# Idle bf16 matmuls moved around the last chunk's projection, and a cast of x1 given to ScalarE

## The reference

```
qkv = x @ w_qkv;  q, k = rope(rmsnorm(q)), rope(rmsnorm(k))
o   = softmax(q k^T / sqrt(8)) v
x   = layernorm(x + o @ w_proj + b_proj)                    # called x1 in the kernel
h   = silu((x @ w1) * s1) * ((x @ w2) * s2)                 # 128 -> 512
h   = gelu((h @ h1) * t1);  h = gelu((h @ h2) * t2)         # 512 -> 512, twice
out = layernorm(x + (h @ w3) * s3)                          # 512 -> 128
```

## Time and profile before

| | |
|---|---|
| three runs | 388.29, 390.14, 392.93 us; median 390.14 us |
| the profiled execution, its own time | 389.85 us |
| its span, first to last instruction | 388.1 us |
| mean granted TensorE clock over the span | 0.976 |
| busy share of the span | PE 87%, ACT 79%, DVE 52%, PEld 35%, POOL 5% |
| chain that ended last | PE 60%, ACT 17%, DVE 12%, issue 9% |

### The profile page before, as it was taken

One profiled execution on the slowest core, in us unless ns is written; L12 is line 12 of the kernel. 1 busy time (PEld: TensorE's weight loads), 2 busy tenths in 40 slices (PEclk: granted clock), 3 DMA queues, 4 the chain that ended last, 5 costly groups with the idle time before them and its releaser, 6 DMA issues.

```text
span 388.1 us, 6219 instructions
## 1 busy us (share of the span) xinstructions
PE 338.2 (87%) x2093; PEld 136.5 (35%) x2098; DVE 202.5 (52%) x397; ACT 306.1 (79%) x347; POOL 18.4 (5%) x21
## 2 busy tenths in 40 slices
PE   8976488878799999998999989998999899969980
PEld 3533111111132244533322444433223535425750
DVE  1899927101145754354556634455477153665754
ACT  2566399999999989797999888889998987852430
POOL 2300000000010000001100000011000000021001
PEclk9999699999999999999999999999999999988997
DMA  7998933123033030020302300303031100000001
GB/s 246 345 375 276 380 128 96 32 66 98 5 93 93 6 98 0 19 79 2 123 29 68 96 0 0 96 0 125 0 96 52 45 0 0 0 27 0 0 2 32
DMA packets 16201, 31.33 MB, mean 81 GB/s; under 512 B 1522, under 2 KB 5106, under 8 KB 16178
## 3 DMA queue, kind: packets, MB, share of 16 engines
q1 hardware_dynamic: 15938, 30.23, 23.8%
q0 software_dynamic: 240, 0.79, 0.5%
HBM read 19.21 MB, written 9.44 MB: 74 GB/s over the span
## 4 chain that ended last, share of the span: by engine, by line
PE 60%; ACT 17%; DVE 12%; issue 9%; ACTq 0%; POOLq 0%; DVEq 0%; POOL 0%
PE ps L456 20%; ACT probs L718 16%; PE ps L503 14%; PE ps L443 10%; PE ps L493 4%; PE ps L584 4%; DVE ffn L898 2%; PE ps L537 2%; DVE probs L805 2%; DVE parts L794 2%; PE ps L632 1%; PE ps L616 1%; PE ps L416 1%; PE ps L473 1%; DVE x_lo L873 1%
## 5 line engine op out<-in xcount | busy, mean ns | idle before, releaser
L718 ACT ACTIVATE probs<-ps 128x1024 f32<-128x1024 f32 x256 | 241.3, 1051 | 29.8 <-PE ps L443 29.7
L456 PE MATMUL ps<-probs,va 128*9 128x512 f32 x1024 | 130.3, 598 | 14.3 <-ACT probs L718 12.7
L443 PE MATMUL ps<-qa,ka 32*128 32x512 f32 x512 | 74.5, 501 | 11.7 <-ACT probs L718 7.0
L443 PEld LDWEIGHTS ps<-qa,ka 32*128 32x128 f32 x512 | 29.9, 184 | 108.7 <-ACT probs L718 68.7
L898 DVE TENSOR_SCALAR ffn<-ps,col 128x512 f32<-128x512 f32 x36 | 27.0, 750 | 55.1 <-PE ps L503 50.9
L503 PE MATMUL ps<-g_hi,w_hi 128*128 128x512 f32 x108 | 45.4, 421 | 2.5 <-DVE ffn L898 2.5
L503 PE MATMUL ps<-g_lo,w_hi 128*128 128x512 f32 x108 | 42.4, 392 | 0.0
L456 PEld LDWEIGHTS ps<-probs,va 128*9 128x9 f32 x1024 | 17.8, 89 | 62.3 <-ACT probs L718 32.5
L835 DVE STREAM_TRANSPOSE o_tok<-ps 128x512 f32<-128x512 f32 x15 | 10.7, 716 | 44.8 <-PE ps L456 44.8
L503 PEld LDWEIGHTS ps<-g_hi,w_hi 128*128 128x128 f32 x108 | 20.2, 187 | 15.4 <-DVE ffn L898 4.3
L873 DVE TENSOR_TENSOR g_lo<-ffn,g_hi 128x512 fp32r<-128x512 f32 x36 | 24.9, 692 | 1.2
(11 more groups left out here) (103 smaller groups left out, 290.6 us busy)
## 6 DMA issues: line engine op xcount, KB each, us to landing
ka<-k_scr SPq DMA_DIRECT2D x16, 512.0 KB, 4.1
qa<-q_scr SPq DMA_DIRECT2D x16, 256.0 KB, 4.1
q_scr<-parts SPq DMA_DIRECT2D x6, 512.0 KB, 6.4
k_scr<-parts SPq DMA_DIRECT2D x6, 512.0 KB, 6.7
va<-v_all SPq DMA_DIRECT2D x16, 144.0 KB, 4.5
ffn<-in_h SPq DMA_DIRECT2D x2, 1024.0 KB, 8.7
xT<-in_x_t SPq DMA_DIRECT2D x4, 256.0 KB, 4.9
q_scr<-rope SPq DMA_DIRECT2D x2, 512.0 KB, 7.1
```

What stands on the lines that cost most here:

```text
L443: mm = pe.matmul(s_tile(u)[:, i, :], ka[rows, slot, kt * P:(kt + 1) * P], qa[rows, slot, :], start=True, stop=not shifted)
L456: mm = pe.matmul(ps[32 * h:32 * h + VW, O_BANK, :], va[:, g % 2, kt, h, :], probs[:, step % 4, h, :], start=(kt == 0), stop=(kt == KT - 1))
L718: nc.scalar.activation(probs[:, step % 4, 2 * pair:2 * pair + 2, :], s_tile(u), ACT.Exp).then_inc(exp_done, 1)
```

## The change

The idle matmuls are spread over six places in place of two: `KEEP_WARM = (5, 6, 2, 10, 2, 3)`. Five go ahead of the last value matmuls, six behind them, two behind the first half of the projection, ten behind its second half (ahead of the turn of x1, where 14 were), two behind the first half of the turn, three behind its second. The wait on `mix_free` that stood behind the projection now stands ahead of the last value matmuls. The cast into `x_hi` goes from DVE to ACT, behind the preload of the Silu table; DVE waits for it (`last_x_high`) and does the subtraction alone. `G_SPLIT` is still counted up by DVE's subtractions.

```diff
-KEEP_WARM = (14, 6)
+KEEP_WARM = (5, 6, 2, 10, 2, 3)
...
+        last_x_high = sem("last_x_high")
...
-                def turned(step, bank0, src):
+                def turned(step, bank0, src, after=(0, 0)):
 
                     for hf in range(2):
                         pe.wait_ge(last_given, step + hf + 1)
                         for i in range(HT):
                             mm = pe.transpose(ps[:, bank0 + hf, i * P:(i + 1) * P], src(hf * HT + i), ident[:])
                         mm.then_inc(last_ready, 1)
-
+                        keep_warm(after[hf])
+
+                pe.wait_ge(mix_free, MIX_CHUNK * (NCH - 1) + MIX_FIRST)
+                keep_warm(KEEP_WARM[0])
                 values(c, STEPS - 1)
+                keep_warm(KEEP_WARM[1])
                 for hf in range(2):
                     pe.wait_ge(last_given, G_ATTN + hf + 1)
                     for i in range(HT):
                         mm = pe.matmul(ps[:, 4 + hf, i * P:(i + 1) * P], attnT[:, (hf * HT + i) * P:(hf * HT + i + 1) * P], wp[:],
                                        start=True, stop=True)
                     mm.then_inc(last_ready, 1)
-                pe.wait_ge(mix_free, MIX_CHUNK * (NCH - 1) + MIX_FIRST)
-                keep_warm(KEEP_WARM[0])
-                turned(G_X, 0, lambda i: x1[:, i, :])
-                keep_warm(KEEP_WARM[1])
+                    keep_warm(KEEP_WARM[2 + hf])
+                turned(G_X, 0, lambda i: x1[:, i, :], KEEP_WARM[4:6])
                 pe.wait_ge(last_given, G_SPLIT + 2)
...
             act.preload_act_table(ACT.Silu)
+            for hf in range(2):
+                act.wait_ge(last_ready, R_X + hf + 1)
+                nc.scalar.copy(x_hi[:, hf * HC:(hf + 1) * HC], ps[:, hf, 0:HC]).then_inc(last_x_high, 1)
...
             for hf in range(2):
-                dve.wait_ge(last_ready, R_X + hf + 1)
-                split(cb, ps[:, hf, 0:HC], half_of(x_hi, hf), half_of(x_lo, hf)).then_inc(last_given, 1)
+                dve.wait_ge(last_x_high, hf + 1)
+                nc.vector.tensor_tensor(half_of(x_lo, hf), ps[:, hf, 0:HC], half_of(x_hi, hf).bitcast(F32), ALU.subtract).then_inc(last_given, 1)
```

## The result

Over 22 runs of each, the changed kernel has a median of 388.7 us (386.66 to 390.91), the kernel before 391.11 us (388.29 to 393.24). The medians are 2.4 us apart; the ratio is 0.9941, 95% interval 0.9918 to 0.9963, which is 2.3 us less, 0.6%. This is more than the noise of so many runs, and less than the 1% that a few could tell. The forecast was 2.45 us less, as 387.7 us from a median of 390.14 that three runs gave; 19 more runs put that median 1 us higher, and the range of 385.9 to 390.1 holds 388.7.

The account below looks back on a forecast made before the run. Idle matmuls ahead of the turn of x1, lengthened by a halved clock, were taken to bound the tail. Removing them and casting on ACT moves the first FFN product from 355.66 to 353.21: 390.14 - 2.45 = 387.7 us, range 385.9 to 390.1.

Parts of the forecast that it names:

- The main term: Ahead of the turn of x1: the whole idle block leaves the path; first FFN product 2.45 us sooner in all.
- rival 3: Behind the value matmuls: clock falls anyway, idle matmuls delay projection and turn; first product 2.8 us later, 392.9 us; chance 0.07.
- Five ahead of the last value matmuls: Five idle matmuls fill a 1.08 us hole before the last value matmuls; delay taken as 0, bounds 0 and 0.25 us.
- Projection at the full clock: First half of the projection takes between 0.61 and 1.22 us at full clock, 0.61 being nearer.
- A faster projection gains nothing: Projection behind the values: finishing sooner saves 0 us, as DVE is not ready for it before 348.86.
- The cast: Cast of turned x1 into x_hi on ACT: 0.40 us each, gaining 0.4 us over a cast on DVE.
- Three in place of six behind the turn: Idle matmuls behind the turn of x1: 0.65 us from 352.25, clear of the first product at 353.21.
- The signs: Profile after: clock 1.00 from 342 to 380, DVE order kept, casts about 0.40 us, first product 9.5 us behind last exp.
- The table load for the copies: ACT's casts of x1 might bring a 1.28 us table load, in idle time or ending as the first Silu is due.
- Rival 1: Clock falls anyway between projection and turn of x1: gain only 0.45 us, time 389.7 us; chance 0.12.
- Rival 2: Clock falls around the turn of x1, FFN products 3.4 us longer: 0.95 us slower, 391.1 us; chance 0.08.
- Rival 4: Idle block before the turn: all 14 at low clock take 6.0 us elsewhere, so gain 3.6 us, 386.5 us; chance 0.11.

Follow-up runs that it names:

- second profile of before: The unchanged kernel profiled a second time: 11.35 us from last exp's end to first FFN product, 391.93 us whole time.
- none at the values: Changed kernel without the eleven idle matmuls around the last value matmuls: last exp to first FFN product 9.97 and 9.93 us; 389.69 us, ratio to before 0.9947.
- cast on ACT alone: Kernel before with only the cast given to ACT, KEEP_WARM (14, 6) kept: last exp to first FFN product 11.64 us; 389.85 us, ratio 0.9967.
- none at all: Changed kernel without any idle matmul in the tail: last exp to first FFN product 9.71 us; 391.35 us, ratio to before 1.0001.
- fourteen, covered: Changed kernel with 14 idle matmuls in place of ten ahead of the turn of x1: last exp to first FFN product 9.51 us; 388.79 us.
- high part first, one idle: Changed kernel, x1 turned into banks 4 and 5, two x_hi products before the last subtraction, one idle matmul behind the turn, not three: 388.34 us, ratio 0.9927.
- none at the turn: Changed kernel without the five idle matmuls in and behind the turn of x1: 390.62 us in one profile, 388.63 us in the second.

## Why the prediction was right, by its own steps

**The main term.** The block of idle matmuls was on the path before, and isn't after. The forecast had the first product 2.45 us sooner; the first profiles give 12.00 - 9.43 = 2.57, against the second profile of before it is 1.92. The reading of *why* the block was long holds as well: all six profiles without idle matmuls at the values (before twice, none at the values twice, cast on ACT alone, none at all) have a low clock ahead of the first product, and all eight with them have none there. In fourteen, covered, the old count costs 9.51, so of the 2.57 us the count itself is 0.08, the cast 0.24, and some 2.2 is left for the clock together with what it does to the block's length.

That sharing out holds only from this end. Taken from the other, with the clock left to fall, the shorter block and the cast already give 2.0 of the 2.57 us (none at the values, 9.97 and 9.93). Part of this may be the execution: in those two the clock was low for 3.4 us, in the first profile of before for 6.8. Against the second profile of before, which was also low for 3.4 us, it is 1.4 us. No run has fewer idle matmuls in the old places and nothing else changed. The two parts of the change do much the same job twice, so neither has a share of its own. The prediction did not say that: it priced a fall with the new counts as rival 3, up to 2.8 us slower. In both profiles such a fall cost 0.5 us, since the clock was back before most of the ten were issued. The later rise that rival 3 needed was not met in any run with ten ahead; it stays open whether it can be.

**The cover of each hole.** Five ahead of the last value matmuls: these began at 345.57, 0.08 behind E, and before 0.04 behind it (343.70). Between the bounds of 0 and 0.25 I took 0; it is 0.04 against before. Six behind: the projection starts 1.50 us behind the value matmuls, as before (1.51). Projection at the full clock: 0.71 us for a half, near the 0.61 that I took. "A faster projection gains nothing" was 0.1 us off: the sum over the first half now begins 0.08 before the transpose ahead of it is listed as ended (349.34 against 348.97 + 0.45), where before it began with that end, at 347.56, the slow first half of the projection having ended only at about 347.5. From the end of the value matmuls to x1's second half it is 6.85 us and was 6.97. That is 0.12 us, as much as the stretch beat the forecast by; the 0.04 us lost ahead of the values came back behind x1, where 1.45 us to the first product were forecast and 1.41 measured.

**The cast.** 0.37 us against 0.40. Its worth over a cast on DVE was put at 0.4 and is 0.24, as DVE overlaps its own instructions: two splits at 0.92 each were taken for 1.76 us, though the rows of before already had both between 353.93 and 355.62, in 1.69. This is the most mis-sized number of the prediction. The sum doesn't rest on it, since it goes by the path over ACT.

**Three in place of six behind the turn.** No cost found in either form.

**The signs.** Those that stand on the path came as written: the values right behind the five idle matmuls, DVE's order, the turn released by DVE, the casts at 0.37 us, the first product at 9.43. No DVE wait for PE stands at the residual sum (L1038 now). One sign fails by its letter: the granted clock is 0.56 of the stretch 379 to 380, so it fell at 379.12. PE's last instruction had ended at 378.75, and before the clock fell there as well, at 383.12; no matmul is left to pay for it.

**The rivals.** The table load for the copies didn't come: ACT's two casts stand 0.56 us apart with nothing between. Rival 1 (a fall between projection and turn) happened in no profile with cover. Rival 2 (a fall around the turn) was a mechanism to be taken seriously: it did not occur with the five idle matmuls there, and did occur in one of two profiles without them, at 1.6 us and not the 3.4 priced. It did not occur in the six profiles with cover that have five idle matmuls at the turn, or three (high part first, one idle); six against two are few to say that these prevent it. The Trainium skill's "TensorE: Matmul & The Clock Gate" ("Part 4: PE-mode transpose") says that transposes don't count as PE activity in the same way as matmuls. With transposes and pauses alone the granted clock here was 1.00 through the turn in both profiles and fell behind it in one. That is neither proof nor refutation of the rule, since the pauses may have done it. Rival 4 (14 at the low clock all the way, 6.0 us) was not seen; the three blocks took 4.35 to 4.78.

## What to carry to other kernels

Filler work that keeps TensorE's clock up belongs into the holes where PE waits anyway, sized to end before the wait does: there ten or fourteen cost 0.0 to 0.1 us, while each one that stands in the queue when its successor's input is ready costs its full 0.216 us (they stand 0.43 apart if the clock has already fallen). Look for its price and its use together: no filler at all took the same time as filler in the wrong place (391.35 and 391.55 us). And measure from an event behind which the change lies, since the last exp ended at 343.66 and at 346.15 us in the two profiles of the kernel before, as much apart as the whole effect.

## What the runs showed of the hardware

The clock fell without any long pause. In the first profile of before PE had stood idle for 1.08 us ahead of the last value matmuls and for 0.8 us behind them (344.79 to 345.57) when the clock fell; the pause went on to 346.30, so the 1.5 us that the prediction counts as lying ahead of the fall were half over. In the first profile of none at the turn PE's pauses behind the ten were 0.28, 0.50 and 0.92 us, and the clock fell 0.94 us into the products, while PE was busy. In the second profile of the kernel before, the same instruction stream lost the clock 2.5 us later behind the same event (E + 4.4 against E + 1.9). It stayed low for 3.4 us in some profiles and for 6.8 in others. One kernel (none at the turn) kept it in one execution and lost it in the other. So a kernel with such holes has a tail that differs by 1.6 us between executions, with nothing changed.

The same clock goes with part of the difference ahead of the tail. From the start of the span to E it stood at 0.50 for 6.8 us in two of the fourteen profiles, with E at 343.06 and 343.66; for 10.2 us in eight, with E between 344.01 and 345.77; and for 13.7 us in four, with E between 345.43 and 347.12. In the second profile of before four products of the first part of the kernel (L416) take 3.27 us at the low clock, where they took 1.98 in the first. No run here changes that part, so what filler would give there is open.

At the low clock four fp32 instructions of the projection took 1.22 us, at the full clock 0.71: less than a factor of two.
